# A two-layer decoder on one core: the second expert's gate and up products ahead of the first routing row, and two pieces of VectorE work in another order

## The chip, the cores and the metric

The kernel runs on one core of one Trainium2 chip. The metric is the device time of one execution, in microseconds; the time before is 1000.16 us, the median of three runs (999.84 to 1000.23).

## What is computed

The program is a decoder of two layers on 2 x 1024 tokens of width 256. Each layer is an attention, a cross attention to a context of 154 rows and a feed-forward block, each behind a layer norm and added to `x`. The change lies in the feed-forward block of the first layer, a mixture of 8 experts with hidden width 128, of which each token takes 2:

```python
def _L0_ffn_ref(hidden_states, gate_weight, e_score_correction_bias, gate_proj, up_proj, down_proj):
    ...
    topk_idx, topk_weight = _gate(xf, gate_weight.astype(jnp.float32), e_score_correction_bias.astype(jnp.float32))
    y = jnp.zeros_like(xf)
    for e in range(E):
        combine_w = jnp.where(topk_idx == e, topk_weight, 0.0).sum(-1)
        g = xf @ gate_proj[e].T
        u = xf @ up_proj[e].T
        o = jax.nn.silu(g) * u @ down_proj[e].T
        y = y + combine_w[:, None] * o
    return y.reshape(Bv, Sv, Hv)
...
x = x + _L0_ffn_ref(_layernorm(x, axis=-1), ...)
x = x + _L1_attn_ref(_layernorm(x, axis=-1), ...)
```

`_gate` takes sigmoid scores plus a bias, keeps the two best of four groups, then the two best experts, and normalises their weights.

## The kernel before

All stages run one behind the other on the five engines, with a barrier between stages. The order on each engine is written out by hand, and semaphores tie the engines together. The stage of the change is `experts` (from L2159). It computes all 8 experts for all tokens, in 4 rows of 512 tokens; number n is row n // 8, expert n % 8. Every fp32 operand is kept as two float16 parts, high and low, so a product takes three matmuls for each half of 256 features.

For each n TensorE does `gate_up(n)`: 6 matmuls of 512 columns into `psg` (gate), 6 into `psu` (up, both L2311), and one into the single bank `psc` (L2321), which spreads the routing weights of expert e over 128 partitions. Then `project(n - 2)` does 12 matmuls with the down weights into `acc` (L2332). ScalarE does `gate` (silu of `psg`, L2268) and `high` (the float16 cast, L2274). VectorE does `product` (two multiplications, L2217 and L2218; the second one reads `psc` and raises `h_ready`), and `low` one expert later (the low part `hp`, L2224). `psc` of n may not be written before `h_ready` n.

Routing of a row: `variances` (L820 to L833, VectorE), `power` (L811, GpSimd), `offsets` (L838), the normalised tiles (L852, L857 on VectorE, L846 on ScalarE), their transposes (L864), `logit`, `scores`, then on VectorE `groups` (L2140 to L2144) and `choice` (L2128 to L2156), which ends with the weights `mr_cw`. TensorE turns them (`turn_weights`, L2120), ScalarE copies them into `cwT` (L2103), and only then can a row's first `psc` be made. For rows 1 to 3 this is spread over the row before, by `STATS_AT, TILES_AT, LOGITS_AT, GROUPS_AT, CHOICE_AT = 0, (1, 2), 3, 5, 6`: expert 0 has the statistics, 1 and 2 the tiles, 5 the groups, 6 the choice. The routing of row 0 is at the head of the stage.

`lent.low` 4 and 5 (L2060, `gw_down<-gw_raw,gw_down`) make the low parts of the down weights. `project(0)` waits for them, and so does the sync engine: `ahead.load` issues the next stage's weights into the same buffer `gw_raw`,

```python
        @block.sync
        def _(sp):
            sp.wait_ge(lent.low_done, 6)
            ahead.load(sp, ins)
```

after which GpSimd folds a row into them: `ahead.fold`, three pairs of subtractions of 512 columns (L2462, L2463), each with two operands in SBUF. ScalarE and VectorE split these weights into parts at fixed experts (`on_scalar`, `on_vector`: L2551 at expert 3 of row 0, L2556 at expert 7, and later).

Of the kernel before, what the change touches and what calls it, by code (L numbers as in the profile page):

```python
# [2001 lines left out]
NE = 8  # L2002
WSCALE = 64.0
NBLK, BT = 4, 512
# [154 lines left out]
def experts(nc, x, ins, lent, ahead, routes):  # L2159

    with ExitStack() as ctx:
# [7 lines left out]
        id16, cwT, pick = lent.id16, lent.cwT, lent.pick  # L2169
# [4 lines left out]
        psg, psu, psc = ps("psg", [P, 2, BT]), ps("psu", [P, 2, BT]), ps("psc", [P, 1, BT])  # L2174
# [3 lines left out]
        psw = shared.bitcast(F16)[0:2 * NE, 0:BT]  # L2178
# [4 lines left out]
        g_ready, u_ready, silu_done, h_ready, hi_done = sem("g_ready"), sem("u_ready"), sem("silu_done"), sem("h_ready"), sem("hi_done")  # L2183
        parts_done, down, added = sem("parts_done"), sem("down"), sem("added")
        STATS_AT, TILES_AT, LOGITS_AT, GROUPS_AT, CHOICE_AT = 0, (1, 2), 3, 5, 6
        block = ctx.enter_context(nc.Block())
# [5 lines that stand above are left out]
# [14 lines left out]
        @block.vector  # L2206
        def _(v):
            own = Tally(v, s_v)
            L = own.link

            def product(n):
                k = n % 2
                v.wait_ge(silu_done, n + 1)
                v.wait_ge(u_ready, n + 1)
                if n >= 2:
                    v.wait_ge(parts_done, n - 1)
                L(v.tensor_tensor(h[:, k, :], sg[:, k, :], psu[:, k, :], ALU.mult))  # L2217
                v.tensor_tensor(h[:, k, :], h[:, k, :], psc[:, 0, :], ALU.mult).then_inc(h_ready, 1)  # L2218

            def low(n):  # L2220
                v.wait_ge(hi_done, n + 1)
                if n >= 3:
                    v.wait_ge(down, n - 2)
                v.tensor_tensor(hp[:, n % 3, 1, :], h[:, n % 2, :], hp[:, n % 3, 0, :], ALU.subtract).then_inc(parts_done, 1)  # L2224

            def add(b):
                v.wait_ge(down, (b + 1) * NE)
                for j in range(4):
                    ins_ = v.scalar_tensor_tensor(x[:, 4 * b + j, :], acc[:, j, :], 1.0 / WSCALE, x[:, 4 * b + j, :], ALU.mult, ALU.add)
                ins_.then_inc(added, 1)  # L2230

            v.wait_ge(lent.made, 5)
            routes.groups(v, own, 0, lent)
            routes.choice(v, own, 0, lent)
            lent.low(v, 4)
            lent.low(v, 5)
            for n in range(NBLK * NE):
                b, e = n // NE, n % NE
                product(n)
                if n:  # L2240
                    low(n - 1)
                if e == 1 and b:
                    add(b - 1)
                if b + 1 < NBLK:
                    if e == STATS_AT:
                        routes.variances(v, own, b + 1)
                    if e == TILES_AT[0]:
                        routes.offsets(v, b + 1)
                    if e in TILES_AT:
                        routes.low(v, own, 2 * (b + 1) + TILES_AT.index(e))  # L2250
                    if e == GROUPS_AT:
                        routes.groups(v, own, b + 1, lent)
                    if e == CHOICE_AT:
                        routes.choice(v, own, b + 1, lent)
                ahead.on_vector(v, own, (b, e), added, turned_ps)
            low(NBLK * NE - 1)
            add(NBLK - 1)
# [41 lines left out]
        @block.tensor  # L2299
        def _(t_):  # L2300
            mm = t_.matmul
            t_.wait_ge(lent.made, 5)

            def gate_up(n):
                b, e, k = n // NE, n % NE, n % 2
                for w, d, s in ((gw, psg[:, k, :], g_ready), (uw, psu[:, k, :], u_ready)):
                    if n >= 2:
                        t_.wait_ge(silu_done if w is gw else h_ready, n - 1)
                    for c in range(2):
                        for px, pw in ((0, 0), (0, 1), (1, 0)):  # L2310
                            last = mm(d, w[:, pw, 1024 * c + P * e:1024 * c + P * e + P], routes.block(b)[:, 2 * px + c, :],  # L2311
                                      start=(c + px + pw == 0), stop=(c == 1 and px == 1))
                    if w is gw:
                        last.then_inc(s, 1)
                if n == 0:
                    routes.turn_weights(t_, 0, psw, id16)
                if e == 0:
                    t_.wait_ge(routes.cwT_ready, b + 1)
                if n:
                    t_.wait_ge(h_ready, n)  # L2320
                mm(psc[:, 0, :], pick[:, e, :], cwT[:, BT * b:BT * b + BT], start=True, stop=True).then_inc(u_ready, 1)  # L2321

            def project(n):
                b, e, k = n // NE, n % NE, n % 3
                t_.wait_ge(parts_done, n + 1)
                if n == 0:
                    t_.wait_ge(lent.low_done, 6)
                if e == 0 and b:
                    t_.wait_ge(added, b)
                for j in range(4):  # L2330
                    for ph_, pw in ((0, 0), (0, 1), (1, 0)):
                        last = mm(acc[:, j, :], hp[:, k, ph_, P * j:P * j + P], dw[:, pw, D * e:D * e + D],  # L2332
                                  start=(e == 0 and j % 2 == 0 and ph_ + pw == 0), stop=(e == NE - 1 and ph_ == 1), skip_group_check=True)
                last.then_inc(down, 1)

            t_.wait_ge(lent.low_done, 4)
            gate_up(0)
            gate_up(1)
            for n in range(2, NBLK * NE + 2):
                b, e = (n - 1) // NE, (n - 1) % NE  # L2340
                t = TPB * (b + 1)
                if n < NBLK * NE:
                    gate_up(n)
                if b + 1 < NBLK:
                    if e == TILES_AT[1]:
                        routes.turn(t_, t + 1, psx, id16, t + 1)
                    if e == LOGITS_AT:
                        routes.turn(t_, t + 3, psx, id16, t + 3)
                project(n - 2)
                if b + 1 < NBLK:  # L2350
                    if e in TILES_AT:
                        routes.turn(t_, t + 2 * TILES_AT.index(e), psx, id16, t + 2 * TILES_AT.index(e))
                    if e == LOGITS_AT:
                        routes.logit(t_, b + 1, psl)
                    if e == CHOICE_AT:
                        routes.turn_weights(t_, b + 1, psw, id16)
                if (b, e) == (NBLK - 1, 0):
                    t_.wait_ge(routes.xT_ready, NT)
                ahead.on_tensor(t_, (b, e), turned_ps)
# [1381 lines left out]
```

## Time and profile before

| | |
|---|---|
| time, median of three runs | 1000.16 us |
| the profiled execution: time, span of the trace | 1000.26 us, 998.5 us |
| busy over the span: PE, DVE, ACT, POOL | 84%, 77%, 65%, 38% |
| mean granted clock of TensorE | 0.951 |
| stage of the experts, from the start of the first gate product to the last addition | 351.1 to 502.2 us |

PE is TensorE's matmul, PEld its weight load, DVE VectorE, ACT ScalarE, POOL GpSimd, SP the sync engine. All starts are microseconds from the start of the span. A row of the timeline gives start, duration, engine, line, operation, result and operands, and in brackets how long the engine had been idle and what ended that. A granted clock of 1.00 is the level of 2.4 GHz, 0.50 that of 1.2 GHz.

### The profile page before, as it was taken

The numbers are of one execution on the slowest core, as the hardware profiler recorded it, in microseconds if no ns is written. First come the engines' busy times: TensorE is split into PE (matmuls) and PEld (weight loads), VectorE is DVE, ScalarE is ACT, GpSimd is POOL, SyncE is SP. The second block draws the span as 40 slices with busy tenths as digits, with TensorE's granted clock in tenths as the row PEclk, the third lists the DMA queues.
The fourth block names the chain that finished last, engine by engine and source line by source line (L and its number), as shares of the span: only waits on it lengthen the run. The fifth ranks groups of instructions, "written<-read, shape, count | busy, mean of one in ns | idle before, by whom it ended". The sixth has DMA issues, their size and how long they took to land. (4 is left out here: it accounts for less than half of the span.)

```text
span 998.5 us, 23455 instructions
## 1 busy us (share of the span) xinstructions
PE 840.8 (84%) x9338; PEld 552.9 (55%) x9338; DVE 773.0 (77%) x1434; ACT 653.2 (65%) x1184; POOL 375.1 (38%) x372
## 2 busy tenths in 40 slices
PE   1386879798489889999968999997799987999997
PEld 0122223232156645555535776765699975778786
DVE  7899989934678988888758999984878876667443
ACT  4588688888468544653328888884688866656431
POOL 1043444322237213000027888884334822224220
PEclk9999879899769989999979999999899999999999
DMA  5402324150231030000040000000200000000000
GB/s 152 84 2 36 50 33 55 16 71 1 62 108 43 2 117 21 2 1 1 1 173 2 3 3 3 3 3 12 64 2 2 2 2 1 1 11 12 12 22 33
DMA packets 21675, 30.55 MB, mean 31 GB/s; under 512 B 6000, under 2 KB 17982, under 8 KB 20416
## 3 DMA queue, kind: packets, MB, share of 16 engines
q1 hardware_dynamic: 18816, 26.44, 11.4%
q10 hardware_dynamic: 2752, 2.62, 0.9%
q8 instruction: 75, 1.23, 0.5%
q14 instruction: 32, 0.26, 0.1%
HBM read 18.56 MB, written 2.10 MB: 21 GB/s over the span
## 5 line engine op out<-in xcount | busy, mean ns | idle before, releaser
L589 ACT ACTIVATE t_pT<-t_sc 128x1536 f32<-128x1536 f32 x96 | 137.0, 1454 | 29.2 <-PE t_sc L696 28.9
L269 POOL TENSOR_SCALAR_AFFINE_SELECT t_pT<-t_pT 128x512 f32<-128x512 f32 x64 | 74.3, 1183 | 167.2 <-ACT t_pT L589 167.2
L696 PE MATMUL t_sc<-t_qk 32*128 32x512 f16 (+3 forms) x1152 | 87.0, 358 | 47.6 <-DMA t_qk<-t_sin_parts 26.6
L696 PEld LDWEIGHTS t_sc<-t_qk 32*128 32x128 f16 x1152 | 36.2, 98 | 106.7 <-issue 54.4
L717 PE MATMUL t_ot<-t_pT,t_v 128*17 128x512 f32 (+3 forms) x768 | 79.5, 525 | 12.9 <-DVE t_ou L433 6.1
L2701 POOL TENSOR_SCALAR_AFFINE_SELECT r_att<-r_att 128x1024 f16<-128x1024 f16 x64 | 68.8, 1101 | 26.4 <-DVE r_att L2750 26.4
L1983 PE MATMUL c_pso<-ck_VO,c_pT 128*128 128x256 f16 x480 | 55.0, 273 | 1.4 <-DVE c_pT L1824 1.4
L2268 ACT ACTIVATE m_sg<-m_psg 128x512 f32<-128x512 f32 x32 | 19.1, 596 | 51.6 <-PE m_psg L2311 51.6
L1894 ACT ACTIVATE c_pt<-c_pss,c_mx 128x154 f32<-128x154 f32 x128 | 48.6, 416 | 2.4 <-DVE c_mx L1807 2.4
L1983 PEld LDWEIGHTS c_pso<-ck_VO,c_pT 128*128 128x128 f16 x480 | 46.3, 98 | 6.7 <-DVE c_pT L1824 1.6
L3004 PE MATMUL r_psv<-ra_w,ra_xT 128*128 128x512 f16 x192 | 48.1, 388 | 0.8 <-DVE r_v L2757 0.7
L2332 PE MATMUL m_acc<-gw_down,m_hp 128*128 128x256 f16 x384 | 47.2, 273 | 1.8 <-DVE m_hp L2224 1.4
L2728 POOL TENSOR_TENSOR r_sm<-r_sm,ra_sm 128x16 f32<-128x16 f32 x16 | 46.4, 2900 | 2.6 <-DVE r_sm L2784 2.6
L1774 POOL TENSOR_TENSOR c_pn<-c_pt,c_tot 128x208 f32<-128x208 f32 x16 | 24.1, 1508 | 59.3 <-DVE c_tot L1814 59.3
L717 PEld LDWEIGHTS t_ot<-t_pT,t_v 128*17 128x17 f32 x768 | 17.4, 100 | 51.3 <-issue 36.0
L2332 PEld LDWEIGHTS m_acc<-gw_down,m_hp 128*128 128x128 f16 x384 | 36.9, 98 | 12.4 <-DVE m_hp L2224 2.0
L2750 DVE TENSOR_TENSOR r_att<-r_pss,r_att 128x1024 f16<-128x1024 f32 x32 | 39.0, 1219 | 5.4 <-ACT r_att L2878 5.3
L1905 ACT CAST c_pT<-c_pst 128x512 f16<-128x512 f32 (+1 forms) x48 | 25.3, 529 | 17.9 <-PE c_pst L1973 17.9
L1824 DVE TENSOR_TENSOR c_pT<-c_pst,c_pT 128x512 f16<-128x512 f32 (+1 forms) x48 | 28.7, 598 | 10.3 <-ACT c_pT L1905 9.5
L2311 PE MATMUL m_psg<-m_xT,gw_gate 128*128 128x512 f16 x144 | 35.0, 379 | 0.0
L2311 PE MATMUL m_psu<-m_xT,gw_up 128*128 128x512 f16 x144 | 35.0, 379 | 0.0
L3455 ACT ACTIVATE f_h<-fs_k 128x512 f16<-128x512 f32 x24 | 15.2, 632 | 29.5 <-DVE fs_k L3328 20.1
(600 smaller groups left out, 2422.5 us busy)
## 6 DMA issues: line engine op xcount, KB each, us to landing
t_qk<-t_cos_parts SPq DMA_DIRECT2D x24, 128.0 KB, 5.3
t_qk<-t_sin_parts SPq DMA_DIRECT2D x24, 128.0 KB, 6.9
x<-in_x ACTq DMA_DIRECT2D x4, 512.0 KB, 6.2
out_x<-x SPq DMA_DIRECT2D x8, 256.0 KB, 2.1
r_rcos<-in_ret_cos SPq DMA_DIRECT2D x1, 1280.0 KB, 8.2
r_rsin<-in_ret_sin SPq DMA_DIRECT2D x1, 1280.0 KB, 10.4
t_qk<-t_cos_parts SPq DMA_DIRECT2D x16, 64.0 KB, 2.6
gw_raw<-in_gateT SPq DMA_DIRECT2D x1, 1024.0 KB, 7.6
```

The source lines that it names most:

```text
L269: last = g.affine_select(out=blk, in_=blk, compare_op=ALU.is_ge, fill=0.0, base=0, pattern=[[0, 4], [1, P]], channel_multiplier=-1)
L589: a.activation(pT[:, at:at + 3, :].rearrange("p a s -> p (a s)"), sc[s % 2][:], ACT.Exp, scale=CURVE * CURVE / math.sqrt(2 * DH)).then_inc ...
L696: last = t.matmul(sc[s % 2][:, 512 * k + at:512 * k + at + w], qk[r, g % 3, 1, of_k, P * i:P * i + P], qk[r, g % 3, 0, of_q, q0:q0 + w], s ...
L717: last = t.matmul(ot[j][32 * h:32 * h + DH + 1, 512 - w:512], v1[:, b, 4 * c + h, i, :], pT[:, (4 * slot + h) % RING, at:at + w], start=be ...
L1894: last = a.activation(pt[:, q, h, :], pss[:, k, n * CTX:n * CTX + CTX], ACT.Exp, bias=mx[:, q, 3 * k + n:3 * k + n + 1], scale=1.0, accum_ ...
L1983: last = mm(pso[:, 0:D], l, r, start=(n == 0), stop=(n == len(todo) - 1))
L2311: last = mm(d, w[:, pw, 1024 * c + P * e:1024 * c + P * e + P], routes.block(b)[:, 2 * px + c, :], start=(c + px + pw == 0), stop=(c == 1 ...
L2332: last = mm(acc[:, j, :], hp[:, k, ph_, P * j:P * j + P], dw[:, pw, D * e:D * e + D], start=(e == 0 and j % 2 == 0 and ph_ + pw == 0), sto ...
L2701: last = g.affine_select(out=blk, in_=blk, compare_op=ALU.is_ge, fill=0.0, base=0, pattern=[[0, 8], [1, P]], channel_multiplier=-1)
L2728: g.tensor_tensor(sm[:, q, 2, :], sm[:, q, 1, :], ahead.sm[:, 4, 0:1].broadcast_to((P, HR)), ALU.pow).then_inc(pow_done, 1)
L2750: v.tensor_tensor(att[:, t % 2, 1, 2 * j:2 * j + 2].rearrange("p h g m -> p (h g m)"), pss[:].rearrange("p j m -> p (j m)"), att[:, t % 2, ...
L3004: last = mm(d, l, r, start=(i == 0), stop=(i == len(todo) - 1))
```

## The change

`gate_up` is split. The 12 matmuls are now `products(n)`, and number 1's are issued right behind number 0's, ahead of row 0's `turn_weights` and `psc`. On VectorE the statistics of row 1 move from behind `product(0)` to the place in front of it, where `lent.low` 4 and 5 stood, and those two move behind `low(0)`, inside number 1.

```diff
             routes.groups(v, own, 0, lent)
             routes.choice(v, own, 0, lent)
-            lent.low(v, 4)
-            lent.low(v, 5)
+            routes.variances(v, own, 1)
             for n in range(NBLK * NE):
                 b, e = n // NE, n % NE
                 product(n)
                 if n:
                     low(n - 1)
+                if n == 1:
+                    lent.low(v, 4)
+                    lent.low(v, 5)
                 if e == 1 and b:
                     add(b - 1)
                 if b + 1 < NBLK:
-                    if e == STATS_AT:
+                    if e == STATS_AT and b:
                         routes.variances(v, own, b + 1)
...
             def gate_up(n):
                 b, e, k = n // NE, n % NE, n % 2
+                if n != 1:
+                    products(n)
+                if n == 0:
+                    products(1)
+                    routes.turn_weights(t_, 0, psw, id16)
+                if e == 0:
+                    t_.wait_ge(routes.cwT_ready, b + 1)
+                if n:
+                    t_.wait_ge(h_ready, n)
+                mm(psc[:, 0, :], pick[:, e, :], cwT[:, BT * b:BT * b + BT], start=True, stop=True).then_inc(u_ready, 1)
+
+            def products(n):
+                b, e, k = n // NE, n % NE, n % 2
                 for w, d, s in ((gw, psg[:, k, :], g_ready), (uw, psu[:, k, :], u_ready)):
                     if n >= 2:
                         t_.wait_ge(silu_done if w is gw else h_ready, n - 1)
...
                     if w is gw:
                         last.then_inc(s, 1)
-                if n == 0:
-                    routes.turn_weights(t_, 0, psw, id16)
-                if e == 0:
-                    t_.wait_ge(routes.cwT_ready, b + 1)
-                if n:
-                    t_.wait_ge(h_ready, n)
-                mm(psc[:, 0, :], pick[:, e, :], cwT[:, BT * b:BT * b + BT], start=True, stop=True).then_inc(u_ready, 1)
```

TensorE at the head of the stage, before (`m_psg` and `m_psu` are the gate and up products, `mr_cw` the routing weights, `m_psc` their spread, `m_acc` the down products):

```order
L2311 MATMUL m_psg<-ce_room,gw_gate 128x512 x6
L2311 MATMUL m_psu<-ce_room,gw_up 128x512 x6
L2120 MATMUL m_shared<-gw_id,mr_cw 16x128 x4
L2321 MATMUL m_psc<-gw_cwT,gw_pick 128x512
L2311 MATMUL m_psg<-ce_room,gw_gate 128x512 x6
L2311 MATMUL m_psu<-ce_room,gw_up 128x512 x6
L2321 MATMUL m_psc<-gw_cwT,gw_pick 128x512
```

and now (its lines in the changed kernel are L2326, L2317):

```order
L2326 MATMUL m_psg<-ce_room,gw_gate 128x512 x6
L2326 MATMUL m_psu<-ce_room,gw_up 128x512 x6
L2326 MATMUL m_psg<-ce_room,gw_gate 128x512 x6
L2326 MATMUL m_psu<-ce_room,gw_up 128x512 x6
L2120 MATMUL m_shared<-gw_id,mr_cw 16x128 x4
L2317 MATMUL m_psc<-gw_cwT,gw_pick 128x512 x2
```

Twelve matmuls stand in front of the turn, and the two `psc` products stand one behind the other with nothing between them; nothing moves from number 2 on.

VectorE behind the choice of row 0, before:

```order
L2156 TENSOR_TENSOR mr_cw<-mr_s,mr_cw 128x4x8
L2060 SCALAR_TENSOR_TENSOR gw_down<-gw_raw,gw_down 128x1024 x2
L2217 TENSOR_TENSOR m_h<-m_sg,m_psu 128x512
L2218 TENSOR_TENSOR m_h<-m_h,m_psc 128x512
L820 BN_STATS mr_st<-x 128x6 x4
...
L833 TENSOR_SCALAR mr_sm<-mr_sm 128x4
L2217 TENSOR_TENSOR m_h<-m_sg,m_psu 128x512
L2218 TENSOR_TENSOR m_h<-m_h,m_psc 128x512
L2224 TENSOR_TENSOR m_hp<-m_h,m_hp 128x512
L838 SCALAR_TENSOR_TENSOR mr_sm<-mr_sm 128x4
```

and now:

```order
L2156 TENSOR_TENSOR mr_cw<-mr_s,mr_cw 128x4x8
L820 BN_STATS mr_st<-x 128x6 x4
...
L833 TENSOR_SCALAR mr_sm<-mr_sm 128x4
L2217 TENSOR_TENSOR m_h<-m_sg,m_psu 128x512
L2218 TENSOR_TENSOR m_h<-m_h,m_psc 128x512
L2217 TENSOR_TENSOR m_h<-m_sg,m_psu 128x512
L2218 TENSOR_TENSOR m_h<-m_h,m_psc 128x512
L2224 TENSOR_TENSOR m_hp<-m_h,m_hp 128x512
L2060 SCALAR_TENSOR_TENSOR gw_down<-gw_raw,gw_down 128x1024 x2
L838 SCALAR_TENSOR_TENSOR mr_sm<-mr_sm 128x4
```

The statistics are first, the products of numbers 0 and 1 follow each other, and the two `gw_down` instructions are last. The same instructions stand between the choice and `offsets` (L838) as before. The order on ScalarE, GpSimd and the sync engine is unchanged.

## Rows read from the trace of the kernel before

**Rows 1.** Page, busy time by engine.

```profile
PE 840.8 (84%) x9338; PEld 552.9 (55%) x9338; DVE 773.0 (77%) x1434; ACT 653.2 (65%) x1184; POOL 375.1 (38%) x372
```

**Rows 2.** Stretches: length, busy PE, PEld, DVE, ACT, POOL, granted clock, DMA share, GB/s.

```profile
349.00:351.30 2.30, 0.33 (x6) 0.15 (x3) 0.94 (x3) 0.75 (x3) 0.40 (x3) 1.00 0.00 0
351.30:354.70 3.40, 3.40 (x10) 1.15 (x9) 3.09 (x12) 1.69 (x3) 2.06 (x5) 0.50 0.00 0
354.70:358.10 3.40, 1.33 (x9) 0.54 (x8) 3.09 (x12) 0.57 (x1) 0.00 (x0) 1.00 0.00 0
365.00:388.90 23.90, 23.90 (x181) 14.92 (x178) 20.44 (x43) 13.75 (x23) 8.91 (x6) 1.00 0.27 95
388.90:392.00 3.10, 2.09 (x14) 0.95 (x13) 2.89 (x10) 0.63 (x2) 0.00 (x0) 1.00 0.00 0
```

**Rows 3.** Timeline of PE.

```profile
357.99 0.49 PE L2321 MATMUL m_psc<-gw_cwT,gw_pick 128*128 128x512 f16 x1 [0.67 <-ACT gw_cwT L2103]
365.51 1.47 PE L2332 MATMUL m_acc<-gw_down,m_hp 128*128 128x256 f16 x12
379.18 0.38 PE L2321 MATMUL m_psc<-gw_cwT,gw_pick 128*128 128x512 f16 x1
387.41 0.38 PE L2321 MATMUL m_psc<-gw_cwT,gw_pick 128*128 128x512 f16 x1
390.11 0.39 PE L2120 MATMUL m_shared<-gw_id,mr_cw 128*16 128x128 f16 x4 [1.01 <-DVE mr_cw L2156]
```

**Rows 4.** Timeline of DVE, head of the stage.

```profile
356.79 2.35 DVE L2060 SCALAR_TENSOR_TENSOR gw_down<-gw_raw,gw_down 128x1024 f16<-128x1024 f32 x2
359.06 0.68 DVE L2217 TENSOR_TENSOR m_h<-m_sg,m_psu 128x512 f32<-128x512 f32 x1
360.38 1.40 DVE L820 BATCH_NORM_STATS2 mr_st<-x 128x6 f32<-128x256 f32 x4
363.21 0.69 DVE L2217 TENSOR_TENSOR m_h<-m_sg,m_psu 128x512 f32<-128x512 f32 x1
365.14 0.15 DVE L838 SCALAR_TENSOR_TENSOR mr_sm<-mr_sm 128x4 f32<-128x4 f32 x1
367.05 0.68 DVE L2217 TENSOR_TENSOR m_h<-m_sg,m_psu 128x512 f32<-128x512 f32 x1
```

**Rows 5.** Timeline of SP (first issue of the loads) and of POOL (the folds).

```profile
359.17 0.37 SPq L2432 DMA_DIRECT2D gw_raw<-in_L_attn_o_w  x1
...
372.92 1.32 POOL L2462 TENSOR_TENSOR gw_raw<-gw_raw 128x512 f32<-128x512 f32 x1 [8.97 <-DMA gw_raw<-in_L_attn_g_w]
...
377.64 1.72 POOL L2463 TENSOR_TENSOR gw_raw<-gw_raw 127x512 f32<-127x512 f32 x1
380.55 1.28 POOL L2463 TENSOR_TENSOR gw_raw<-gw_raw 127x512 f32<-127x512 f32 x1
```

**Rows 6.** Timeline of DVE, numbers 4 to 7.

```profile
376.56 1.68 DVE L2224 TENSOR_TENSOR m_hp<-m_h,m_hp 128x512 f16<-128x512 f32 x1
379.66 0.69 DVE L2217 TENSOR_TENSOR m_h<-m_sg,m_psu 128x512 f32<-128x512 f32 x1 [1.42 <-PE m_psc L2321]
380.98 1.39 DVE L2224 TENSOR_TENSOR m_hp<-m_h,m_hp 128x512 f16<-128x512 f32 x1
382.30 0.18 DVE L2140 TENSOR_TENSOR mr_sc<-mr_s,mr_bias 128x32 f32<-128x32 f32 x1
384.30 0.69 DVE L2217 TENSOR_TENSOR m_h<-m_sg,m_psu 128x512 f32<-128x512 f32 x1
```

**Rows 7.** Timeline, POOL and DVE, small DVE instructions beside POOL's.

```profile
327.92 2.77 POOL L2055 TENSOR_SCALAR gw_down<-gw_raw 128x1024 f16<-128x1024 f32 x1
327.57 0.16 DVE L827 TENSOR_TENSOR mr_sm<-mr_sm 128x4 f32<-128x4 f32 x1
533.47 2.14 POOL L2701 TENSOR_SCALAR_AFFINE_SELECT r_att<-r_att 128x1024 f16<-128x1024 f16 x2 [1.84 <-DVE r_att L2750]
534.66 0.99 DVE L2783 SCALAR_TENSOR_TENSOR r_sq<-r_sq,r_rfloor 128x16 f32<-128x16 f32 x1
```

## The prediction

> **What bounds the kernel now.** The page comes first: no engine is busy throughout, PE is the fullest with 84% [rows 1], so the stage of the change has to be read by itself. The table of stretches shows what limits it [rows 2]. From 365.0 to 388.9 PE is busy for 23.90 of 23.90 us: there the stage is PE's. In front of that it is not: from 354.7 to 358.1 PE works 1.33 of 3.40 us while DVE works 3.09. The timeline of PE shows how the head of the stage reaches the steady part: `psc` of number 0 at 357.99, the first down product at 365.51 [rows 3]. The timeline of DVE shows the same time from the other side [rows 4]: from 356.79, the end of row 0's choice, DVE has work with hardly a gap until `product(2)` at 367.05. So both engines are full in the head of the stage, and the change relieves only one of them. The last place to see is where PE next waits: 1.01 us for row 1's routing weights, at 390.11 [rows 3]. This wait ends when DVE is done with row 1's choice, so at that point the stage goes by DVE, and whatever DVE loses between 365 and 390 is lost to the kernel.
>
> **The head of the stage.** Removed from the path of PE: 12 products of 512 columns, which stood behind `psc` of number 0 and now run while DVE computes the choice. PE's part alone would be ready early. DVE's work from 356.79 on is the same instructions in another order, and I add it up from their starts [rows 4]. The statistics take 2.83 us (360.38 to 363.21) and end at 359.6. `psc` of number 0 is made behind the twelve products, the turn and the copy, at about 359.4, so it is just in time. `product(0)` takes 1.32 us to the next start and its result is there at 361.0. Now comes a wait that was not there: `psc` has one bank, so number 1's is made only then, and from a `psc` to the product behind it is 0.48 us (379.18 to 379.66) [rows 3, 6]. `product(1)` starts at 361.5. It and `low(0)` take 1.93 us (363.21 to 365.14), to 363.45. The two `gw_down` instructions take 2.27 us, to 365.7, and end at 365.8. `product(2)` follows 1.91 us behind `offsets` (365.14 to 367.05), at 367.6 for 367.05. The first down product needs `gw_down`: 365.85 for 365.51. PE had the second expert's products out of the way, but it then waits for the low parts, and the head is 0.3 to 0.6 us longer. Should the granted clock fall to 0.50 in PE's pause from 359.4 to 361.0, number 2's twelve products end at about 365.8 and still lie under this wait.
>
> **What is queued behind the moved low parts.** The sync engine waits for both `gw_down` instructions before it issues the next stage's weights. The first issue was at 359.17, at their end [rows 5]; it will be at 365.8, 6.65 us later. The last load lands, and the folds on POOL start, at 379.55 for 372.92. No consumer of the weights is late: the first fixed reader is DVE at expert 7 (after 391). What changes is the neighbour. While POOL's folds run, DVE's instructions with two operands in SBUF stand still. `low(4)` took 1.39 us instead of 0.68, and its last 0.68 us begin at 381.69, 0.14 us ahead of the end of POOL's L2463 (381.83) [rows 5, 6]. In turn the L2463 from 377.64 waited for `low(3)`, which ended at 378.24, and was done 1.12 us later; so a fold holds the port for about 1.0 us. `product` reads PSUM and isn't held (0.69 us at 379.66, beside a fold). In the trace of before the six folds meet three DVE instructions, all on slack of PE's stretch.
>
> Now they meet `groups`. `product(5)` comes at 380.2 (PE is 0.6 us late). Folds 1 and 2 (379.55 and 380.8) pass beside it; `low(4)` arrives at 381.55, in fold 2, and waits 0.4 us. Then DVE has seven small instructions with two SBUF operands in a row, L2140 to L2144, broken by two reductions, and four folds are left. DVE and POOL take turns, and each fold costs DVE about 1.0 us. Undisturbed, `groups` would take 2.0 us (382.30 to 384.30) and `product(6)` start at 381.55 + 0.6 + 2.0 = 384.15. With 0.4 + 4 x 1.0 it is 388.55; if two small instructions slip through between two folds and the reductions run beside one, 388.0. I take 388.3, 4.0 us behind 384.30 [rows 6]. PE's `psc` of number 7, at 387.41 before, needs the end of `product(6)` and waits from 388.0 to 389.7. The choice follows `low(5)`, and from `product(6)` to the turn of the weights is DVE's work alone: 390.11 - 384.30 = 5.81 us, so 394.1. From there every instruction is where it was, 4.0 us later. The 0.6 us of the head is inside this, not beside it: PE's arrival at the turn, 0.6 us later, would have been covered by its wait of 1.01 us.
>
> **Unknown: how small instructions fare beside a fold.** No row has L2140 to L2144 beside one. From below: L827, two operands, 0.16 us in the last half microsecond of POOL's L2055, not held at all. That would give nothing per fold. From above: L2783, 128x16, took 0.99 us inside POOL's selects, and ended with the second of them (535.61) [rows 7]; the smallest of its 16 cases is 0.173 us. That gives the whole rest of an instruction, up to 1.27 us each. I take 1.0, since L2783 and `low(4)` are alike in kind and both ended with POOL's instruction, while L827 met only the tail of one.
>
> The Trainium skill (SBUF: State Buffer, who interferes with whom) says that a DVE instruction with two SBUF inputs and a GpSimd instruction that reads SBUF exclude each other, and that the one that issues first keeps the ports for the whole instruction. The rows agree on the exclusion, and have the release 0.14 us before the end. By the page's whole instruction the four folds would cost 4 x 1.27 us, and the time would be 1.1 us higher, as an estimate.
>
> **The sum.** 1000.26 us for the profiled execution, plus 0 at the end for the head (hidden), plus 4.0 for the folds over `groups`: 1004.3. The median of the runs, 1000.16, is 0.1 us lower than the profiled one, which I leave out. About 0.2% (2 us) is what a measurement of this kernel can tell from no change.
>
> **Rivals.**
> *The folds hurt nobody (chance 0.20, not slower).* If small instructions slip past POOL as L827 did, or the loads land some 3.5 us sooner than their old distance says, `product(6)` starts at 384.4, when its `psc` is there, and the turn of row 1 is at 390.2 to 390.4. The head's delay disappears in PE's wait. Time 1000.4, up to 1001 with the head's 0.6 us. It decides at about 0.2 us of total delay in `groups`: the choice is what PE waits for already, so less than one fold's hold is enough to undo this case. For it speaks L827, against it `low(3)`, `low(4)` and L2783. A lesser form, in which one to three folds are met, gives 1001.5 to 1003.4 (0.08).
> *The folds, and a fall of the clock on top (0.25).* PE would work about 1.7 us between 388.0 and 394.1. The granted clock fell after 0.33 us of work in 2.3, and after 1.33 in 3.4; it stayed with 2.09 in 3.1 [rows 2]. Here the pauses are 1.7 and 2.4 us, between these. A fall lasted 3.4 us at 0.50, and when PE is full that costs 1.7 us: 1006.0.
> *Faster (0.05).* If VectorE weren't full in the head, PE would reach the first down product at about 364.1, 1.4 us earlier, and if the folds hurt nobody and the wait at 390.11 shrank too, the time would be 998.9 at best. Rows 4 speak against it: DVE has no gap to give.
>
> **The numbers.** The forecast itself has 0.42 (1003.5 to 1005.0), the clock's fall 0.25 (1005 to 1006.7), fewer folds 0.08, no harm 0.20, faster 0.05. Range 1000.4 to 1006.4: it leaves out the faster case and the top of the fall. Faster by over 0.2% (below 998.2): 0.05. Within: 0.20. Slower: 0.75.
>
> **What would show it.** First `gw_down` at 363.4; first load issue at 365.8; folds from 379.5; L2140 to L2144 stretched from 0.2 to about 1.2 us, four times; `product(6)` near 388.3; the turn near 394.1, with an idle of over 2 us before it; everything from there 4.0 us later. The forecast is wrong if the small instructions keep 0.2 us beside POOL, if the folds start well before 378, or if PE passes the turn before 392.

## The result, and the profile after

The changed kernel takes 1003.85 us (median of 15 runs) against 1000.23 us for the kernel before (median of 15). The ratio is 1.0029, with a 95% interval of [1.0019, 1.0039]: 2.9 us slower, between 1.9 and 3.9.

The profiled execution takes 1005.03 us with a span of 1003.3 us, 4.8 us over that of before. Not all of this belongs to the change. The first gate product starts at 352.75 for 351.09, and nothing in front of it was edited. So times inside the stage are given from here on from the first gate product of the same trace. On that scale the stage ends (last addition to `x`) at 154.40 for 151.09, 3.31 us later.

TensorE after, from its timeline. The lines answer to [rows 3]:

```profile
352.75 2.47 PE L2326 MATMUL m_psg<-ce_room,gw_gate 128*128 128x512 f16 x6 [1.98 <-PEq L51]
...
362.76 0.39 PE L2317 MATMUL m_psc<-gw_cwT,gw_pick 128*128 128x512 f16 x1 [1.61 <-DVE m_h L2218]
362.99 2.47 PE L2326 MATMUL m_psg<-ce_room,gw_gate 128*128 128x512 f16 x6
...
367.69 1.47 PE L2340 MATMUL m_acc<-gw_down,m_hp 128*128 128x256 f16 x12
...
390.71 0.39 PE L2317 MATMUL m_psc<-gw_cwT,gw_pick 128*128 128x512 f16 x1 [0.81 <-DVE m_h L2218]
391.31 1.49 PE L2340 MATMUL m_acc<-gw_down,m_hp 128*128 128x256 f16 x12 [0.21 <-DVE m_hp L2224]
395.06 0.39 PE L2120 MATMUL m_shared<-gw_id,mr_cw 128*16 128x128 f16 x4 [2.26 <-DVE mr_cw L2156]
```

The first down product stands at 14.94 (14.42 before). The turn of row 1 stands at 42.31 (39.02 before), and in front of it are two new waits, 0.81 and 0.21 us, and a longer old one, 2.26 for 1.01 us. Part of the delay is older than these waits: `product(5)` already starts 0.66 us late (29.23 for 28.57), which comes from the head. All that is lost at the end of the stage (3.31) is lost by this turn (3.29).

VectorE and GpSimd, the lines that answer to [rows 5, 6]:

```profile
379.95 1.27 POOL L2470 TENSOR_TENSOR gw_raw<-gw_raw 128x512 f32<-128x512 f32 x1 [17.93 <-DMA gw_raw<-in_L_attn_g_w]
381.17 1.27 POOL L2471 TENSOR_TENSOR gw_raw<-gw_raw 127x512 f32<-127x512 f32 x1
382.40 1.27 POOL L2470 TENSOR_TENSOR gw_raw<-gw_raw 128x512 f32<-128x512 f32 x1
383.63 1.72 POOL L2471 TENSOR_TENSOR gw_raw<-gw_raw 127x512 f32<-127x512 f32 x1
385.31 1.26 POOL L2470 TENSOR_TENSOR gw_raw<-gw_raw 128x512 f32<-128x512 f32 x1
386.54 1.25 POOL L2471 TENSOR_TENSOR gw_raw<-gw_raw 127x512 f32<-127x512 f32 x1
```

```profile
383.31 0.91 DVE L2224 TENSOR_TENSOR m_hp<-m_h,m_hp 128x512 f16<-128x512 f32 x1
384.14 1.25 DVE L2140 TENSOR_TENSOR mr_sc<-mr_s,mr_bias 128x32 f32<-128x32 f32 x1
385.43 1.18 DVE L2142 TENSOR_TENSOR mr_grp<-mr_sc 128x16 f32<-128x16 f32 x1
386.64 1.24 DVE L2128 TENSOR_TENSOR mr_gt<-mr_grp 128x64 f32<-128x64 f32 x1
387.92 0.23 DVE L2129 TENSOR_TENSOR mr_gt<-mr_gt,gw_after 128x64 f32<-128x64 f32 x1
...
389.25 0.69 DVE L2217 TENSOR_TENSOR m_h<-m_sg,m_psu 128x512 f32<-128x512 f32 x1
```

Before, the second and the third of the small ones took, beside no fold:

```profile
382.51 0.18 DVE L2142 TENSOR_TENSOR mr_grp<-mr_sc 128x16 f32<-128x16 f32 x1
382.72 0.22 DVE L2128 TENSOR_TENSOR mr_gt<-mr_grp 128x64 f32<-128x64 f32 x1
```

Three instructions of 128 partitions by 16 to 64 elements take 1.18 to 1.25 us, where 0.18 to 0.22 us was their time before. Each of them is held by one of the last three folds. When the folds are over, at 387.79, L2129 takes 0.23 us. `product(6)` starts at 36.50 for 33.21.

### The profile page after: what moved, and what is told of

The parts are those of the page before. It is cut to its first block and busy times, and to the rows that moved or that the text cites. A ratio compares the mean times of both kernels' runs of the same rounds, so it can differ in the third digit from the quotient of the medians.

```text
span 1003.3 us, 23455 instructions
## 1 busy us (share of the span) xinstructions
PE 844.0 (84%) x9338; PEld 554.0 (55%) x9338; DVE 774.7 (77%) x1434; ACT 652.7 (65%) x1184; POOL 374.4 (37%) x372
## 5 line engine op out<-in xcount | busy, mean ns | idle before, releaser
L2217 DVE TENSOR_TENSOR m_h<-m_sg,m_psu 128x512 f32<-128x512 f32 x32 | 22.0, 686 | 18.2 <-PE m_psc L2317 11.4
L2326 PE MATMUL m_psg<-m_xT,gw_gate 128*128 128x512 f16 x144 | 35.0, 379 | 0.0
L2326 PE MATMUL m_psu<-m_xT,gw_up 128*128 128x512 f16 x144 | 35.0, 379 | 0.0
```

## Experiments

Every experiment carries two theories. A: the low parts of the down weights come later, so the loads and the folds do too, and the folds hold the small instructions of `groups`. B: the loss is TensorE's own (its pause behind the early products, the granted clock there) or lies in the new order itself. Each was timed in five rounds against the kernel before on the same chip. A run scatters by some us in parts of the program that no edit touches, so the times from the first gate product are the finer measure, though each comes from a single profile; both are given at the end in one table.

**1. Only TensorE's half** (`products(1)` ahead of the turn, VectorE as before).

```diff
             routes.choice(v, own, 0, lent)
-            routes.variances(v, own, 1)
+            lent.low(v, 4)
+            lent.low(v, 5)
...
-                if n == 1:
-                    lent.low(v, 4)
-                    lent.low(v, 5)
```

> Only TensorE's half of the change: the second expert's products ahead of the turn; VectorE's order as before. Theory A (the folds on GpSimd fall on the small instructions of row 1's groups, because the low parts of the down weights come 6.7 us later): the low parts end where they did, the first load is issued and the folds start at their old places (about 8 and 22 us behind the first gate product), L2140 to L2144 keep 0.17 to 0.25 us, and the turn of row 1 is within 0.5 us of before's 39.0 us behind the first gate product; time 0 to 0.5 us over before. Theory B (the loss is TensorE's: its pause behind the early products, the fall of the granted clock on number 2's products): the turn is 2 to 3 us later here too, and the time 3 us over before.

Measured: ratio 0.9997 [0.9986, 1.0008]. The loads are issued at 8.09, as before, and no instruction of `groups` is held. The turn is at 39.99, though, 1.0 us late and outside what A allowed. In this profile the loads landed sooner and the folds ran from 19.76. There they held a normalised tile on which TensorE's next transposes rest:

```profile
372.68 1.83 DVE L857 TENSOR_TENSOR ce_room<-ce_room 128x256 f16<-128x256 f32 x2 [0.57 <-DVE ce_room L852]
```

It took 0.92 us in the traces of both kernels. The fold isn't the whole of the 1.0 us. Twelve more products stand ahead of the turn, so the first `psc` comes at 8.01 for 6.90, and VectorE, which had no gap there before, waits 0.46 us; `product(2)` is 0.57 us late (16.53 for 15.96) before any fold has begun. In time TensorE's half alone can't be told from the kernel before. In its profile it gains nothing: the stage ends 0.97 us later.

**2. Only VectorE's half.**

```diff
-            lent.low(v, 4)
-            lent.low(v, 5)
+            routes.variances(v, own, 1)
...
+                if n == 1:
+                    lent.low(v, 4)
+                    lent.low(v, 5)
...
-                    if e == STATS_AT:
+                    if e == STATS_AT and b:
```

> Only VectorE's half: statistics first, low parts of the down weights inside number 1; TensorE's order as before. Theory A: number 1's product now waits for its psc at 363.0 (in the times of before), the low parts end at 367.3, the first load is issued 8 us later, three or four folds fall on low(4) and the groups, each holding a small instruction for about 1.0 us, product(6) starts 4 to 5 us later and the turn is 43 to 44 us behind the first gate product; time 4 to 5 us over before. Theory B: no loss of the folds' kind; the first down product is 1.8 us later, of which the wait at the turn covers 1.0: 0.8 us over before.

Measured: 1.0057 [1.0035, 1.0079], 5.7 us slower. Loads at 16.20, folds from 28.46, three small instructions held (1.25, 1.17, 1.24 us), turn at 43.56: as A had it. The stage ends 6.2 us late, though, 1.7 us more than the turn, and there the granted clock is the reason (below). The early products of the change are thus worth something: they let the low parts end at 14.8 instead of 16.2, and the turn is 1.25 us earlier with them (42.31 for 43.56). That the stage ends 2.9 us earlier isn't all theirs, since 1.7 us of it is the clock in this one profile.

**3. The kernel before, with the folds moved by one wait.**

```diff
                 if b == 1:
+                    g.wait_ge(parts_done, 4)
                     for j in range(3):
                         ahead.fold(g, j)
```

> The kernel before with one added wait on GpSimd: the folds start behind low(3) (number 4), about 26 us behind the first gate product; nothing of the change is in it, and all loads are issued at their old time. Theory A: two folds pass beside the product of number 5, the others hold low(4) and about three small instructions of the groups for 1.0 us each; the turn is 42.0 to 42.5 us behind the first gate product, and the time is 2.5 to 3.5 us over before, as the change's. Theory B: the time is that of before, within 0.5 us.

Measured: 1.0044 [1.0027, 1.0062]. Nothing of the change is in this kernel, and it loses 4.4 us. Folds from 25.71, `low(4)` 1.32 us, L2140 1.26, L2142 1.17, the rest undisturbed; `product(6)` at 35.22 and the turn at 41.03, 1 us sooner than expected since only two small instructions were caught. Yet the time is above the 2.5 to 3.5 us that A allowed. The stage ends at 154.76, 1.7 us later than the turn accounts for. The stretches show why (busy PE, granted clock, then DMA):

```profile
390.64:394.64 4.00, 2.36 (x16) 1.00 0.00 0
394.64:398.64 4.00, 2.97 (x11) 0.67 0.00 0
398.64:402.64 4.00, 4.00 (x25) 0.91 0.00 0
```

Behind TensorE's waits for `psc` and for the turn the clock fell to the lower level. In the changed kernel's profile it stayed, in nearly the same place:

```profile
388.75:392.75 4.00, 2.98 (x19) 1.49 (x17) 3.79 (x10) 1.11 (x2) 0.00 (x0) 1.00 0.00 0
392.75:396.75 4.00, 1.74 (x12) 0.87 (x12) 3.66 (x13) 0.57 (x1) 0.00 (x0) 1.00 0.00 0
396.75:400.75 4.00, 4.00 (x26) 2.39 (x25) 3.64 (x7) 2.06 (x3) 0.00 (x0) 1.00 0.00 0
```

**4. The same, 3 us later still**: `g.wait_ge(u_ready, 6)` in place of `parts_done, 4`.

> As folds_mid, with the folds about 1 to 2 us later: GpSimd waits for number 5's psc, 28.5 us behind the first gate product. Theory A: low(4) falls into the second fold and the other four all fall on the groups, so five instructions are held for about 1.0 us each; product(6) is 37 to 37.5 us and the turn about 43 us behind the first gate product (39.0 before), 4 us over before. Were the loss set by something of fixed size that goes with any added wait on GpSimd, it would be that of folds_mid.

Measured: 1.0066 [1.0048, 1.0084]. This is the clearest picture of the hold. Two timelines, POOL and DVE:

```profile
382.42 1.72 POOL L2463 TENSOR_TENSOR gw_raw<-gw_raw 128x512 f32<-128x512 f32 x1
384.10 1.26 POOL L2464 TENSOR_TENSOR gw_raw<-gw_raw 127x512 f32<-127x512 f32 x1
385.32 1.26 POOL L2463 TENSOR_TENSOR gw_raw<-gw_raw 128x512 f32<-128x512 f32 x1
386.55 1.26 POOL L2464 TENSOR_TENSOR gw_raw<-gw_raw 127x512 f32<-127x512 f32 x1
```

```profile
381.30 1.71 DVE L2225 TENSOR_TENSOR m_hp<-m_h,m_hp 128x512 f16<-128x512 f32 x1
382.93 1.25 DVE L2140 TENSOR_TENSOR mr_sc<-mr_s,mr_bias 128x32 f32<-128x32 f32 x1
384.22 1.18 DVE L2142 TENSOR_TENSOR mr_grp<-mr_sc 128x16 f32<-128x16 f32 x1
385.43 1.24 DVE L2128 TENSOR_TENSOR mr_gt<-mr_grp 128x64 f32<-128x64 f32 x1
386.70 1.18 DVE L2129 TENSOR_TENSOR mr_gt<-mr_gt,gw_after 128x64 f32<-128x64 f32 x1
387.92 0.22 DVE L2130 TENSOR_REDUCE mr_cnt<-mr_gt 128x16 f32<-128x64 f32 x1
```

Four folds, four small instructions, strictly one for one, and none slips through. `product(6)` is at 37.60, the turn at 43.42 (expected 37 to 37.5 and about 43). The time was a miss: 4 us were expected, 6.6 [4.8, 8.4] measured. The stage of the profile ends 4.4 us late, and that is the fastest of the six runs; the rest isn't located.

**5. The changed order, with the folds back in their old place.** The weights that lie in the gate and up buffers are loaded behind the fourth low part, the subtracted rows behind the sixth.

```diff
-            sp.wait_ge(lent.low_done, 6)
-            ahead.load(sp, ins)
+            sp.wait_ge(lent.low_done, 4)
+            ahead.load(sp, ins, lent)
...
+        n = 0
+        sp.wait_ge(lent.low_done, 6)
+        for nm, w in (("q", 256), ("k", 256), ("v", 512), ("g", 512)):
+            sp.dma_start(self.last[:, n:n + w], ins[f"L1_attn_{nm}_w"][D - 1:D].broadcast_to((P, w))).then_inc(self.s_last, 16)
+            n += w
...
                 if b == 1:
+                    g.wait_ge(parts_done, 3)
```

> The changed kernel with the folds put back to their old place: the weights that only need the gate and up buffers are loaded behind the fourth low part, the rows that the folds subtract behind the sixth, and GpSimd waits for low(2). The order on TensorE and VectorE is the changed one. Theory A: the folds run from about 21 to 30 us behind the first gate product, pass before the groups or touch them with one fold at most, L2140 to L2144 lose 0 to 1.0 us, and the turn is 39.0 to 40.3 us behind the first gate product; time 0 to 1.2 us over before, 2 to 3.3 us under the change. Theory B: the time stays that of the change, 3 us over before.

Measured: 1.0010 [0.9997, 1.0022]; folds from 22.78, no small instruction held, turn at 39.92.

**6. Its counterpart: the kernel before with the same wait**, `g.wait_ge(parts_done, 3)`.

> The kernel before with the folds tied to low(2) of number 3, so that a varying landing of the loads can't move them. Theory A: the folds run from 22 to 31 us behind the first gate product as in the profile of before, the turn is at 39.0 to 39.3 us, the median is within 1 us of before's, and, if the landing of the loads is what spreads the runs of before over 6 us (in the profile of pe_only the folds began 2 us earlier and held a normalised tile), the runs lie closer together: within 3 us. If the spread comes from elsewhere it stays at 5 to 6 us.

Measured: 1.0005 [0.9992, 1.0018]. Folds 22.78 to 31.62, turn 39.92, stage end 152.02. Experiment 5 has 22.78 to 31.63, 39.92 and 152.01. With the folds in one place, the two orders end the stage at the same moment. But in this the clock had a part, for the head of experiment 6 isn't that of the kernel before:

```profile
357.07 0.59 PE L2120 MATMUL m_shared<-gw_id,mr_cw 128*16 128x128 f16 x4 [3.09 <-DVE mr_cw L2156]
366.37 1.47 PE L2333 MATMUL m_acc<-gw_down,m_hp 128*128 128x256 f16 x12
```

In the profile of before the first twelve products ran at a granted clock of 0.56 to 0.59, and it was 1.00 when the turn came. Here they ran at 1.00, TensorE then waited 3.09 us, and the clock was 0.50 from 357.23 to 361.23, under number 1's products. The first down product is at 15.14 therefore (14.42 before, 14.94 in experiment 5), and `product(5)` at 29.25, as in experiment 5. Two heads of equal length were compared, equal by luck. The pair shows that behind the head the two orders run alike; it doesn't show that the new head costs nothing, and experiments 7 to 10 show that it costs 0.6 to 0.7 us.

The second expectation fell: the runs lie between 996.2 and 1003.6, spread as before. The landing of the loads isn't what scatters them.

**7 and 8. Folds of 8 columns**, in the changed kernel and in the one before. Left out is the subtraction from the other 504 columns of each third.

```diff
-        c = slice(512 * j, 512 * j + 512)
+        c = slice(512 * j, 512 * j + 8)
```

> The changed kernel with folds of 8 columns instead of 512: the subtraction of the last row from the other 504 columns of each third of the weights is left out; all loads, waits and orders stay. Theory A: the loads land as late as in the changed kernel, but nothing is held; product(6) waits only for its psc, the turn of row 1 is 39.0 to 39.3 us behind the first gate product (42.3 in the changed kernel), time within 0.5 us of before. Theory B (late weights, or the order itself): still 3 us over before.

> The same on the kernel before, with the same part left out. Theory A: low(3), the split at expert 3 and low(4) are no longer held, product(6) waits for its psc and starts 0.5 us earlier; the turn is 38.5 us behind the first gate product, time 0.5 us under before and 0.5 us under after_short_folds: all that is left of the change is its longer head.

Measured: 1.0001 [0.9987, 1.0015] and 0.9998 [0.9987, 1.0009]. In the first the loads are as late as in the change (14.82) and the folds start at 27.37, but

```profile
380.90 0.21 POOL L2470 TENSOR_TENSOR gw_raw<-gw_raw 128x8 f32<-128x8 f32 x1 [18.09 <-DMA gw_raw<-in_L_attn_g_w]
384.70 0.18 DVE L2140 TENSOR_TENSOR mr_sc<-mr_s,mr_bias 128x32 f32<-128x32 f32 x1
```

and the turn is at 39.29. It isn't the lateness of the weights that costs: it is GpSimd's time on the port. Between the two kernels the turn and the stage end differ by 0.68 us (151.36, 150.68), the longer head. Both have the same wait at the turn, 0.59 us, so the wait doesn't cover it. The runs can't resolve that difference.

**9 and 10. Choice one expert earlier.** The turns wait for VectorE's choice, so this edit moves groups to expert 4 and the choice to 5, and the folds behind row 1's choice.

```diff
-        STATS_AT, TILES_AT, LOGITS_AT, GROUPS_AT, CHOICE_AT = 0, (1, 2), 3, 5, 6
+        STATS_AT, TILES_AT, LOGITS_AT, GROUPS_AT, CHOICE_AT = 0, (1, 2), 3, 4, 6
...
-                    if e == CHOICE_AT:
+                    if e == CHOICE_AT - 1:
                         routes.choice(v, own, b + 1, lent)
...
                 if b == 1:
+                    g.wait_ge(routes.cw_ready, 2)
```

> The order of before, with the next row's groups at expert 4 and its choice at expert 5 on VectorE (5 and 6 before; TensorE's turn stays at 6), and the folds behind row 1's choice. Theory A (the turn waits for VectorE's choice, which the folds can reach or not): the waits of 1.0, 0.6 and 0.6 us at the three turns go, the folds hold only low(5) and low(6); the turn of row 1 is 37.9 to 38.9 us behind the first gate product for 39.0, and the time 1.3 to 2.4 us under before. If the choice were not what the turn waits for, the time would be before's.

> The same two edits on the changed kernel. Theory A: the loss of 3 us is gone, since the folds no longer stand beside groups, and the head's 0.5 us, which the wait at the turn covered, shows now: the turn of row 1 is 38.4 to 39.4 us behind the first gate product, the time 0.8 to 1.9 us under before and 0.5 us over early_choice. Theory B (the loss is in the changed order itself): 2 to 3 us over early_choice.

Measured: 1.0002 [0.9989, 1.0015] and 1.0001 [0.9989, 1.0013], a miss in time. The waits at the turns did go (turn at 37.97 and 38.60). But the folds now met the readers of their own result, and the additions of row 0 came late, in the timelines of POOL, DVE and PE of experiment 9:

```profile
393.74 1.27 POOL L2463 TENSOR_TENSOR gw_raw<-gw_raw 128x512 f32<-128x512 f32 x1
394.98 1.26 POOL L2464 TENSOR_TENSOR gw_raw<-gw_raw 127x512 f32<-127x512 f32 x1
```

```profile
393.81 1.22 DVE L2557 TENSOR_REDUCE ra_mean<-gw_raw 128x32 f32<-128x1024 f32 x1 [1.16 <-POOL gw_raw L2464]
395.07 1.21 DVE L2558 TENSOR_SCALAR ra_mean<-ra_mean 128x32 f32<-128x32 f32 x1
```

```profile
404.56 1.47 PE L2333 MATMUL m_acc<-gw_down,m_hp 128*128 128x256 f16 x12 [1.63 <-DVE x L2230]
```

The reduction of L2557 runs beside a fold and takes 1.22 us, as it does without one (1.21 before). L2558 has a single operand in SBUF and is held all the same, 1.21 us for 0.18.

For the changed order it did half of what A said: the 3 us are gone, and 10 is 0.66 us behind 9 at the stage's end, but neither is below the kernel before in time.

**11 and 12. The readers moved too.**

```diff
-        if event == (0, 7):
+        if event == (1, 6):
             v.wait_ge(self.folded, 4)
...
-        if event == (1, 3):
-            mean = self.mean[:].rearrange("p (c h) -> p c h", c=2)
...
-        if event == (1, 6):
+        if event == (1, 7):
             self.weights_high(a, 1, 3)
```

> early_choice with the readers of the folded weights moved out of the way: mean and centring at expert 6 of row 1 instead of expert 7 of row 0 and expert 3 of row 1, ScalarE's split of the value weights at expert 7 instead of 6. In early_choice VectorE waited 1.16 us for a fold and had the mean's last step held for 1.0 us, and TensorE then waited 1.6 us for the addition of row 0. Theory A: that wait goes, the stage ends 149.0 to 149.6 us behind its first gate product (150.8 in early_choice, 151.1 before), time 1.5 to 2 us under before. If the fold isn't what made TensorE wait there, it stays at 150.8.

> The same on the changed order. Theory A: 0.5 to 0.7 us behind early_mean, since the head is longer and no wait at the turn covers it: the stage ends 149.6 to 150.3 us behind its first gate product, time 1 to 1.5 us under before and 4 us under the changed kernel.

Measured: 0.9963 [0.9951, 0.9976] for the order of before, and 0.9998 [0.9983, 1.0013] for the changed one. The stages end at 149.46 and 150.33, and TensorE's wait for the additions is 0.15 us:

```profile
401.46 1.47 PE L2333 MATMUL m_acc<-gw_down,m_hp 128*128 128x256 f16 x12 [0.15 <-DVE x L2230]
```

Experiment 11 is the one kernel that is clear of the kernel before on the fast side. Of its 3.7 us the stage shows 1.6 us; the rest isn't located, and it has only five runs. In experiment 12 the stage is as expected but the time isn't: its runs go from 994.9 to 1003.5, and the median shows no gain. That stays open.

All of it in one table, us from the first gate product of each profile; "held" counts small instructions of `groups`, and the last column is the ratio of times with its interval:

| kernel | first load | folds | held | turn of row 1 | stage end | ratio to before |
|---|---|---|---|---|---|---|
| before | 8.08 | 21.83 to 30.74 | 0 | 39.02 | 151.09 | |
| changed | 14.82 | 27.20 to 35.04 | 3 | 42.31 | 154.40 | 1.0029 [1.0019, 1.0039] |
| 1 TensorE's half | 8.09 | 19.76 to 29.08 | 0 | 39.99 | 152.06 | 0.9997 [0.9986, 1.0008] |
| 2 VectorE's half | 16.20 | 28.46 to 36.31 | 3 | 43.56 | 157.32 | 1.0057 [1.0035, 1.0079] |
| 3 before, folds later | 8.08 | 25.71 to 33.57 | 2 | 41.03 | 154.76 | 1.0044 [1.0027, 1.0062] |
| 4 before, later still | 8.09 | 28.58 to 36.43 | 4 | 43.42 | 155.51 | 1.0066 [1.0048, 1.0084] |
| 5 changed, folds back | -0.20 | 22.78 to 31.63 | 0 | 39.92 | 152.01 | 1.0010 [0.9997, 1.0022] |
| 6 before, same place | 8.08 | 22.78 to 31.62 | 0 | 39.92 | 152.02 | 1.0005 [0.9992, 1.0018] |
| 7 changed, short folds | 14.82 | 27.37 to 28.38 | 0 | 39.29 | 151.36 | 1.0001 [0.9987, 1.0015] |
| 8 before, short folds | 8.08 | 20.11 to 21.11 | 0 | 38.61 | 150.68 | 0.9998 [0.9987, 1.0009] |

## Why the prediction was right, point by point

**The sum.** 4.0 us were forecast. The profile has 3.3 us at the turn and at the end of the stage. The ratio gives 2.9 [1.9, 3.9], which leaves the 4.0 just outside; the two medians are 3.6 us apart. The time, 1003.85, is 0.45 us under the forecast 1004.3 and inside the range. On VectorE the 3.29 us are made up of three parts: `product(5)` starts 0.66 us late, from there to `groups` it takes 0.48 us less (2.16 for 2.64, since `low(4)` is held 0.23 us instead of 0.71), and `groups` takes 3.11 us more (5.11 for 2.00). By the number of folds that fell on `groups`, three, this is the lesser form that was given 0.08 (one to three folds, 1001.5 to 1003.4), at its upper end; the forecast itself had four. The mechanism is the forecast one. That the time fell into the forecast's own bracket, 1003.5 to 1005.0, is in part luck.

**The head.** `product(2)` was to be 0.55 us late and the first down product 0.3; they are 0.66 and 0.52 late. Between the end of the statistics and `psc` things went as added up: the new wait for the one bank of `psc` is there, 0.56 us on VectorE. The fall of the granted clock under the wait for the low parts came too (0.51 from 363.25 to 366.75), and the twelve products of number 2 ended just in time, as was said. The 0 for the head in the sum is right only because its 0.6 us was counted on VectorE's side. The reason given, that the wait of 1.01 us at the turn would cover it, is wrong. `product(5)` waits for TensorE's `psc`, so VectorE is late by the head too, and the wait, which ends with VectorE's choice, keeps its length. Without the folds the longer head is there at the turn and at the end of the stage (0.68 us, experiments 7 and 8; 0.63 and 0.66, experiments 9 and 10).

**The loads.** 6.65 us later was forecast, 6.74 measured. But the last load landed 12.4 us behind the first issue, not 13.75, so the folds began at 27.20 instead of 28.46. This is the step that was mis-sized. The distance was taken as fixed from one trace, and that trace was the odd one: in the five other profiles where the landing starts the folds it was 11.7 to 12.6 us.

**The hold.** About 1.0 us per fold: 1.00 to 1.07 (1.18 - 0.18, 1.25 - 0.18, 1.24 - 0.22). Of the two forms offered, every instruction held, or two between two folds, the first is the true one. With folds earlier by 1.26 us one fold fewer fell on `groups`: three instead of four, and `low(4)` lost 0.23 instead of 0.4. Hence `product(6)` at 36.50 instead of 37.2 (388.3 - 351.1). From there to the turn were 5.81 us, as taken from before.

**The rows that were passed over.** L827 did run in the tail of an L2055, but not of the one shown with it: it starts at 327.57, ahead of that one (327.92), in the last 0.4 us of the L2055 before it. And the trace of before did have what was called unknown, a small instruction met by the beginning of one of POOL's:

```profile
325.19 5.51 POOL L2055 TENSOR_SCALAR gw_down<-gw_raw 128x1024 f16<-128x1024 f32 x2
```

```profile
327.97 1.01 DVE L829 TENSOR_SCALAR mr_sm<-mr_sm 128x4 f32<-128x4 f32 x1
329.02 0.16 DVE L830 SCALAR_TENSOR_TENSOR mr_sm<-mr_sm 128x4 f32<-128x4 f32 x1
362.41 0.17 DVE L829 TENSOR_SCALAR mr_sm<-mr_sm 128x4 f32<-128x4 f32 x1
```

L829 starts 0.05 us behind the second L2055 and takes 1.01 us; beside nothing it takes 0.17. L830, with two operands in SBUF, then runs in 0.16 us while POOL's record goes on for another 1.5 us (to 330.69). The profiles of experiments 4, 5 and 6 have the same pair (1.00 or 1.01, then 0.16). So an instruction of 2.77 us on POOL held VectorE for some 0.9 us only, and a fold of 1.27 us for 1.0: the length of POOL's record isn't the length of the hold. What sets it no run here shows. These rows speak against the rival of no harm, for which only L827 spoke.

**The rivals.** That small instructions might slip past the folds is refuted by all of experiments 2 to 4. That lateness itself costs is refuted by 7. The fall of the clock on top wasn't in the changed kernel's profile, but it is real: it stands in the profiles of experiments 2 and 3, at 1.7 us each, which is its forecast price. In experiment 4 the clock fell as well, in a wait of 2.56 us for `psc`, but before the turn, and the wait for the turn, 1.01 us there, covered it. Whether it comes in some runs of the changed kernel isn't shown. The faster case: TensorE's half alone gained nothing (experiment 1). VectorE was full in the head, and with the turn behind twelve more products its first product starts 0.55 us later still (8.52 for 7.97).

The Trainium skill (SBUF: State Buffer, who interferes with whom) states an exclusive lock for the whole instruction, which was to cost 1.27 us a fold. The exclusion is in the traces; the length isn't. The small instructions lost 1.0 to 1.07 us each: they start 0.10 to 0.12 us behind the fold, and run in the last 0.13 to 0.14 us of it. L830 above is further from the rule. The measurement decides.

## What to carry to other kernels

Moving an instruction moves whatever waits for it, on every queue: here two VectorE instructions went back by 6.7 us, and the cost came from a third engine some 17 us behind them. A chain of small VectorE instructions with operands in SBUF is the worst neighbour for GpSimd work on SBUF, because each of them can lose most of a GpSimd instruction (1.0 of 1.27 us here); place such work beside instructions that read PSUM, or tie it to a semaphore so that a load's landing can't choose its place. And before relieving an engine, look whether the other one at that point has any gap to give. A last point is for the comparing of profiles: two single profiles can agree because the clock fell in different places, so look at the head of each before reading the end (experiment 6).

## What was not expected of the hardware

With four folds left and a row of small instructions waiting, the two engines took turns strictly one for one (experiment 4), so VectorE instructions of 0.18 to 0.22 us took 1.2 us each, four times running. A `tensor_scalar` with one operand in SBUF was held as well (L829, L2558), a reduction wasn't (L2557), and POOL's L2055 let VectorE go after about a third of its record. The time from the first issue of the same loads to the last landing was 13.75 us in one profile and 11.7 to 12.6 us in five. And parts of the program that no edit touches differed between profiles: the first gate product started anywhere from 350.8 to 354.7 us, which is more than most of the effects studied here.
